# Graph layers on one core: the expansion's f32 products become three bf16 products each

## The reference

```python
def _spmm(row, col, vals, x):
    msg = vals[:, None] * x[col]
    return jax.ops.segment_sum(msg, row, num_segments=N)

def _layer(x_prev, row, col, vals, W_a, b_a, W_b, b_b):
    h = _spmm(row, col, vals, x_prev)
    z = (h + x_prev) @ W_a.T + b_a + h * x_prev @ W_b.T + b_b
    return jnp.where(z >= 0, z, NEG_SLOPE * z)
x = emb[x_ids]
x1 = _layer(x, ...)
x2 = _layer(x1, ...)
x3 = _layer(x2, ...)
return jnp.concatenate((x, x1, x2, x3), axis=1)
```

## Time and profile before

| | |
|---|---|
| median of 3 runs | 9204.5 us (9197.29 to 9209.96) |
| the profiled execution, its own time | 9172.53 us |
| its span, first to last instruction | 9170.8 us |
| mean granted clock of PE | 0.967 of 2.4 GHz |
| PE busy, share of the span | 8540.0 us, 93% |
| PE's weight loads (PEld) | 7869.9 us, 86% |
| DVE busy | 7440.7 us, 81% |
| POOL busy | 5280.1 us, 58% |
| ACT busy | 4551.0 us, 50% |
| DMA | 1718.93 MB, mean 187 GB/s |

### The profile page before, as it was taken

The page is one execution under the profiler, slowest core; times in us unless marked ns, Lnnn a source line. Parts: engine busy times, 40 slices in busy tenths (PEclk is TensorE's granted clock), DMA queues, the critical chain, the costliest instruction groups (busy, mean ns, idle before and its releaser), DMA issues.

```text
span 9170.8 us, 229058 instructions
## 1 busy us (share of the span) xinstructions
PE 8540.0 (93%) x69832; PEld 7869.9 (86%) x69833; DVE 7440.7 (81%) x11531; ACT 4551.0 (50%) x14200; POOL 5280.1 (58%) x3637
## 2 busy tenths in 40 slices
PE   7799997899995899999999999999999999999999
PEld 4577775677773799999999999999999999999999
DVE  7799996999996888877777788777777888777777
ACT  0799991699993466611112566511112566511112
POOL 8688781488783122278886122288885222388884
PEclk8899998899996899999999999999999999999999
DMA  2211110111119877788886677788887677788886
GB/s 84 38 7 7 7 7 16 11 7 7 7 7 28 189 281 280 279 283 283 285 285 241 233 279 280 276 285 285 285 285 220 252 280 281 277 283 283 285 285 202
DMA packets 1005650, 1718.93 MB, mean 187 GB/s; under 512 B 378356, under 2 KB 429624, under 8 KB 1004920
## 3 DMA queue, kind: packets, MB, share of 16 engines
q0 software_dynamic: 378656, 958.17, 34.9%
q1 hardware_dynamic: 499680, 751.43, 22.6%
q10 hardware_dynamic: 127224, 8.24, 3.2%
HBM read 961.68 MB, written 755.66 MB: 187 GB/s over the span
## 4 chain that ended last, share of the span: by engine, by line
PE 63%; DVE 2%; ACT 2%; issue 1%; DMA 1%; DVEq 0%; ACTq 0%; SPq 0%; POOL 0%; POOLq 0%
PE ps L955 35%; PE ps L946 25%; ACT work L717 2%; DVE hT L1272 1%; PE ps L963 1%; PE ps L983 1%; PE ps L984 1%; DVE work L1325 0%; PE ps L973 0%; ACTq L722 0%; DVEq L1329 0%; DVE work L1210 0%; DMA work<-messages,work 0%; DMA tile_base<-start_base 0%; DMA work<-tile_base 0%
## 5 line engine op out<-in xcount | busy, mean ns | idle before, releaser
L955 PE MATMUL ps<-work 128*128 128x125 f32 x28416 | 3294.0, 278 | 44.3 <-DVE work L1325 40.8
L955 PEld LDWEIGHTS ps<-work 128*128 128x128 f32 x28416 | 3240.0, 192 | 98.3 <-DVE work L1325 65.9
L551 POOL DMA_INDIRECT work<-messages,work x1776 | 2712.7, 1527 | 636.4 <-issue 631.7
L946 PE MATMUL ps<-xb,work 125*128 x21504 | 2450.5, 276 | 96.3 <-ACT work L717 75.9
L946 PEld LDWEIGHTS ps<-xb,work 125*128 125x128 f32 x21504 | 2419.3, 192 | 127.4 <-issue 127.4
L1325 DVE TENSOR_TENSOR work<-work,iota_p 128x1000 f32<-128x1000 f32 x1776 | 2119.5, 1193 | 35.3 <-ACT work L735 35.3
L717 ACT ACTIVATE work<-ps,work 128x128 f32<-128x128 f32 x5376 | 1532.8, 368 | 1113.5 <-PE ps L946 1113.5
L536 POOL PARTITION_BROADCAST work<-work x672 | 556.1, 829 | 2324.9 <-DMA work<-slot_cols 1260.7
L735 ACT ACTIVATE work<-work 128x8 f32<-128x8 f32 x1776 | 534.4, 301 | 2687.2 <-DMA work<-messages,work 2685.5
L843 PEld LDWEIGHTS ps<-hT 128*128 128x128 f32 x12768 | 1485.0, 196 | 302.2 <-ACT stage L648 182.7
L843 PE MATMUL ps<-hT 128*128 128x96 f32 x12768 | 1521.3, 280 | 191.2 <-ACT stage L648 188.0
(11 more groups left out here) (206 smaller groups left out, 4054.5 us busy)
## 6 DMA issues: line engine op xcount, KB each, us to landing
messages<-work SPq DMA_DIRECT2D x2688, 256.0 KB, 2.4
work<-messages,work POOLq DMA_INDIRECT x1776
out_x<-xb SPq DMA_DIRECT2D x150, 125.0 KB
sorted_edges<-stage,run_idx POOLq DMA_INDIRECT x798
work<-slot_cols SPq DMA_DIRECT2D x672, 2.0 KB
work<-lane_places SPq DMA_DIRECT2D x532, 5.2 KB
out_x<-xb ACTq DMA_DIRECT2D x4, 1562.5 KB
sorted_edges<-hT SPq DMA_DIRECT2D x4, 908.0 KB
```

The costliest lines, as they stand in the source:

```text
L551: pool.indirect_dma_start(out=ck[:, n, :, :].rearrange("p h x -> p (h x)"), out_offset=None, in_=flat, in_offset=bass.IndirectOffsetOnAxis ...
L946: last = t.matmul(ps[:, n % PR, j * D:(j + 1) * D], col_hot[:, n % OHR, j * P:(j + 1) * P], x_flat[:, bass.ds(offs[n], D)], start=True, st ...
L955: last = t.matmul(part[n], ck[:, n, j // CH, j % CH * D:(j % CH + 1) * D], sel[:, n % SELB, j, :], start=j == 0, stop=j == CHB - 1)
```

## The change

The f32 product of a 0/1 matrix with rows of x becomes three bf16 products that add up in PSUM. An f32 value is split into three bf16 pieces whose sum is exactly the value: `x_high` is the upper half of each f32 of `xb`, read where it lies (a bf16 view at a step of two); `rest` = x - x_high is written in f32 into `hT`, and its upper half `x_mid` is read in place in the same way; `x_low` = rest - x_mid is written packed, in bf16, into `work`. DVE makes `rest` and `x_low` at the start of each layer in four parts each (SPLITS), and PE waits for all of them (`pieces_ready`).

The 0/1 matrices and the column numbers (in DRAM, in `col_src` and in `col_row`) are bf16. DVE makes the matrices of two groups in one instruction, the ring holds eight groups (three pairs ahead of PE), and `col_row` is a ring of two rows (CR2) instead of four, so that POOL waits for the matrices of the row before the last. Since `hT` holds `rest` during the expansion, it isn't zeroed piece by piece: one memset of 12500 columns follows the last group of a layer, and the block sums wait for it. Some sizes of the work buffer follow from this.

```diff
...
-LEAD = 3
...
+CR2 = 2
...
-ZC = 224
+HSORT = 12544
+HTW = NB * D
+SPLITS = 4
...
-        slot_cols = dram("slot_cols", [SLOTS2], U8)
+        slot_cols = dram("slot_cols", [SLOTS2], BF16)
...
-        hT = sb("hT", [P, ABODIES * ZC])
+        hT = sb("hT", [P, HTW])
...
-        OHR = 4
+        OHR = 8
...
-        col_hot = work[0:BLK, AOH0:AOH0 + OHR * GE].rearrange("c (n s) -> c n s", n=OHR)
-        MSG0 = AOH0 + OHR * GE
...
+        x_flat = xb[:, :, :].rearrange("r n d -> r (n d)")
+        rest = hT[0:BLK, 0:HTW]
+        x_high = x_flat.bitcast(BF16).rearrange("r (e t) -> r e t", t=2)[:, :, 1]
+        x_mid = rest.bitcast(BF16).rearrange("r (e t) -> r e t", t=2)[:, :, 1]
+        x_low = wb[0:BLK, 2 * LO0:2 * LO0 + HTW]
...
-        col_row = wu[:, 4 * CV0:4 * CV0 + CB * BATCH * GE].rearrange("c (h x) -> c h x", h=CB)
+        col_row = wb[:, 2 * CV0:2 * CV0 + CR2 * BATCH * GE].rearrange("c (h x) -> c h x", h=CR2)
...
-        slot_col = wu[0:DP, 0:SPP]
+        slot_col = wb[0:DP, 0:SPP]
...
                 def spread_cols(i, first):
                     for h in range(CB):
                         pool.wait_ge(col_src_in[h], la * (ABODIES * DMA) + i * DMA + DMA)
-                        if not first:
-                            pool.wait_ge(col_hot_ready, la * GROUPS + i * AU + ((h + 1) * BATCH - AU))
+                        if not first or h >= CR2:
+                            pool.wait_ge(col_hot_ready, la * (GROUPS // 2) + i * (AU // 2) + (h + 1 - CR2) * BATCH // 2)
                         taken_up()
-                        g.partition_broadcast(col_row[:, h, :], col_src[h * 32:h * 32 + 1, :], channels=P).then_inc(col_spread[h], 1)
+                        g.partition_broadcast(col_row[:, h % CR2, :], col_src[h * 32:h * 32 + 1, :], channels=P).then_inc(col_spread[h], 1)
 
...
             with pe.Fori(0, LAYERS) as la:
                 pe.wait_ge(xb_ready, la * DSTEPS + 1)
+                pe.wait_ge(pieces_ready, la * SPLITS + SPLITS)
                 pe.sem_inc(pe_layers, 1)
                 with pe.Fori(0, ABODIES) as i:
                     _, offs = nc.values_load_multi_w_load_instructions(
                         group_at[0:1, bass.ds(i * AU, AU)], engines=[mybir.EngineType.PE],
                         min_val=0, max_val=(NB - 1) * D, skip_runtime_bounds_check_because="the table holds offsets of blocks")
                     for n in range(AU):
-                        pe.wait_ge(col_hot_ready, la * GROUPS + i * AU + (n + 1))
+                        if n % 2 == 0:
+                            pe.wait_ge(col_hot_ready, la * (GROUPS // 2) + i * (AU // 2) + (n // 2 + 1))
                         pe.wait_ge(msg_ready[n % 2], la * (GROUPS // 2) + i * (AU // 2) + (n // 2 + 1))
                         for j in range(CH):
-                            last = t.matmul(ps[:, n % PR, j * D:(j + 1) * D], col_hot[:, n % OHR, j * P:(j + 1) * P],
-                                            x_flat[:, bass.ds(offs[n], D)], start=True, stop=True)
+                            at = n % OHR * GE + j * P
+                            for k, piece in enumerate((x_high, x_mid, x_low)):
+                                last = t.matmul(ps[:, n % PR, j * D:(j + 1) * D], col_hot[:, at:at + P],
+                                                piece[:, bass.ds(offs[n], D)], start=k == 0, stop=k == 2)
                         last.then_inc(expanded, 1)
 
                 with pe.Fori(0, BBODIES) as i:
...
             with dve.Fori(0, LAYERS) as la:
                 v.tensor_copy(b_now[:, :], bias[:, 0, bass.ds(la, 1)])
                 v.tensor_copy(w_now[:, :, :], w_sb[:, bass.ds(la, 1), :, :].rearrange("p a k d -> p (a k) d")).then_inc(w_now_ready, 1)
+                dve.wait_ge(x0_got, NB * DMA)
+                dve.wait_ge(xb_ready, la * DSTEPS + 1)
+                W = HTW // SPLITS
+                for c in range(SPLITS):
+                    at = slice(c * W, (c + 1) * W)
+                    v.tensor_tensor(rest[:, at], x_flat[:, at], x_high[:, at], ALU.subtract).then_inc(rest_ready, 1)
+                dve.wait_ge(slots_stored, DMA)
+                for c in range(SPLITS):
+                    at = slice(c * W, (c + 1) * W)
+                    dve.wait_ge(rest_ready, la * SPLITS + (c + 1))
+                    v.tensor_tensor(x_low[:, at], rest[:, at], x_mid[:, at], ALU.subtract).then_inc(pieces_ready, 1)
+
                 def free_message(i, n, first):
 
                     if n >= MR:
                 def make_hot(i, n):
                     if n % BATCH == 0:
                         dve.wait_ge(col_spread[n // BATCH], la * ABODIES + i + 1)
-                    dve.wait_ge(expanded, la * GROUPS + i * AU + (n + 1))
-                    v.tensor_scalar(col_hot[:, n % OHR, :], col_row[0:BLK, n // BATCH, n % BATCH * GE:(n % BATCH + 1) * GE],
+                    dve.wait_ge(expanded, la * GROUPS + i * AU + (n + 2))
+                    v.tensor_scalar(col_hot[:, n % OHR * GE:(n % OHR + 2) * GE],
+                                    col_row[0:BLK, n // BATCH % CR2, n % BATCH * GE:(n % BATCH + 2) * GE],
                                     iota_c[0:BLK, :], None, ALU.is_equal).then_inc(col_hot_ready, 1)
 
                 def expand(i, first, last_body):
-                    for n in range(AU):
-                        if n + LEAD < AU:
-                            make_hot(i, n + LEAD)
+                    for n in range(0, AU, 2):
+                        m = n + OHR - 2
+                        if m < AU:
+                            make_hot(i, m)
                         elif not last_body:
-                            make_hot(i + 1, n + LEAD - AU)
-                        if n % 2:
-                            dve.wait_ge(expanded, la * GROUPS + i * AU + (OHR + n + 1))
-                            free_message(i, n, first)
-                            v.tensor_tensor(msg[:, n % MR, :].rearrange("p (j d) -> p j d", j=CH),
-                                            ps[:, n % PR, :].rearrange("p (j d) -> p j d", j=CH),
-                                            val_of[:, bass.ds(i * (AU * CH) + n * CH, CH)][:, :, None].to_broadcast([P, CH, D]),
-                                            ALU.mult).then_inc(msg_ready[1], 1)
-                    v.tensor_scalar(hT[:, bass.ds(i * ZC, ZC)].rearrange("p (a z) -> p a z", a=2),
-                                    iota_p[:, 0:ZC // 2][:, None, :].to_broadcast([P, 2, ZC // 2]), 0.0, None, ALU.mult).then_inc(h_zeroed, 1)
-
-                for n in range(LEAD):
+                            make_hot(i + 1, m - AU)
+                        dve.wait_ge(expanded, la * GROUPS + i * AU + (OHR + n + 2))
+                        free_message(i, n + 1, first)
+                        v.tensor_tensor(msg[:, (n + 1) % MR, :].rearrange("p (j d) -> p j d", j=CH),
+                                        ps[:, (n + 1) % PR, :].rearrange("p (j d) -> p j d", j=CH),
+                                        val_of[:, bass.ds(i * (AU * CH) + (n + 1) * CH, CH)][:, :, None].to_broadcast([P, CH, D]),
+                                        ALU.mult).then_inc(msg_ready[1], 1)
+
+                for n in range(0, OHR - 2, 2):
                     make_hot(0, n)
                 expand(0, True, False)
                 with dve.Fori(1, ABODIES - 1) as i:
                     expand(i, False, False)
                 expand(ABODIES - 1, False, True)
+                dve.wait_ge(expanded, la * GROUPS + (OHR + GROUPS))
+                v.memset(hT[:, 0:N], 0.0).then_inc(h_zeroed, 1)
 
...
-                dve.wait_ge(h_zeroed, la * ABODIES + ABODIES)
+                dve.wait_ge(h_zeroed, la + 1)
```

More of the change, by code:

```diff
@@ L94 @@
 CQ = 2
-ZC = 224
-assert ABODIES * ZC >= N and ABODIES * ZC == 12544 and TB == 592 and GROUPS % AU == 0 and AU == CB * BATCH and AU % MR == 0
+HSORT = 12544
+HTW = NB * D
+SPLITS = 4
+assert HTW >= N
+assert HSORT <= HTW and TB == 592 and GROUPS % AU == 0 and AU == CB * BATCH and AU % MR == 0
 UNITS = [P, GE]
@@ L110 @@
 ROUND = 12582912.0
+WORKW = 22032
 def graph_layers(nc, ids, row, col, vals, emb, weights, biases, out):
@@ L129, in graph_layers @@
         tile_base = dram("tile_base", [P, TBW])
-        slot_cols = dram("slot_cols", [SLOTS2], U8)
+        slot_cols = dram("slot_cols", [SLOTS2], BF16)
         messages = dram("messages", [CHUNKS + CHB // CH, CH * D + CH])
-        hT = sb("hT", [P, ABODIES * ZC])
+        hT = sb("hT", [P, HTW])
         xb = sb("xb", [BLK, NB, D])
-        work = sb("work", [P, 20560])
+        work = sb("work", [P, WORKW])
         w_sb = sb("w_sb", [P, LAYERS, 2, D])
@@ L198, in graph_layers @@
         iota_bl = wb[:, 2 * IB0:2 * IB0 + OHW].rearrange("p (b l) -> p b l", l=LANES)
-        assert IB0 + OHW // 2 <= 20560
+        assert IB0 + OHW // 2 <= WORKW
         hot = [hb[:, r * LT:(r + 1) * LT] for r in range(HR)]
@@ L210, in graph_layers @@
         in_slot = hT[:, IS0:IS0 + SLOTW].rearrange("p (l c) -> p l c", c=SLOTS)
```

(28 more changed lines are left out.)

1 line of the change is left out of this document (removed).

## The result

The changed kernel takes **9031.67 us** (median of 4 runs, 9028.89 to 9040.14) beside 9202.31 us of the kernel before on the same chip: a ratio of 0.982, with a 95% interval of 0.9808 to 0.9832. It is 171 us faster, inside the range of 8670 to 9095, where a gain of 413 us was forecast.

The account below looks back on a forecast made before the run. PE was taken to bound the expansion, DVE at 85% behind it. Expansion -495, passes +76 and zeroing +6 gave -413 us: 8760 us profiled, 8792 us median; range 8670 to 9095 us.

Parts of the forecast that it names:

- PE's own share: Expansion: 12 bf16 matmuls a group replace 8 f32 records, at 56 ns each; 10.8 us a body instead of 14.6.
- Rival (b): Expansion: weight loads don't hide at 2.4 GHz, 87 ns a matmul, 17.2 us a body, 9648 us; chance 0.10.
- (c): Expansion: two pieces read at a 4-byte step run at half rate, 107 ns; 17.8 us a body, 9749 us; chance 0.05.
- The hole: PE between two bodies: about 2.5 us without issue, 1.55 us covered by queued matmuls, 0.95 us idle.
- rival (a): Expansion: PE sees the whole 2.5 us hole, or broadcasts stop DVE; 13.3 us a body or more, 8993 us; chance 0.20.
- DMA: Expansion's stores: the DMA engines' floor is 0.705 us a group, 11.3 us a body.
- the expansion's term: Three expansions: 168 bodies of 12.1 us, 2033 us, 495 us less than before.
- the column reads: Expansion's DMA: the doubled column reads, 4 KB for four groups, are nothing beside the stores' 256 KB a group.
- DVE, POOL, SP: Expansion, a body: DVE 9.8 to 12.2 us with POOL's broadcasts of 1.4 us; SP 11.3 us, at most 12.1.
- Between the stages: Before each expansion: DVE's eight passes take 27.9 us, adding 28 us in layer 1, 24 in layers 2 and 3; 76 in all.
- The zeroing: After each layer's last message: one DVE memset of 10.8 us, mostly hidden in DVE's idle time; 6 us for three layers.

Follow-up runs that it names:

- e9: The changed kernel with offsets loaded once a layer and SP storing 64 of 512 message columns in layers 2 and 3: 8704.52 us (one run).
- e2: The changed kernel with PE's loop in bodies of 32 groups, one load of 32 offsets each: 9105.36 us, ratio 0.9908.
- e3: The changed kernel with DVE writing 64 of the 1024 columns of each pair of 0/1 matrices: 9024.92 us (one run).
- e4: The changed kernel with SP storing 64 of 512 message columns in layers 2 and 3: 8865.14 us (one run).
- e5: The changed kernel with a body's 16 offsets loaded four at a time: 8872.21 us, ratio 0.9664.
- e8: The changed kernel with a body's 16 offsets loaded eight at a time: 8904.44 us, ratio 0.9701.
- e1: The changed kernel with PE's 16 offsets loaded once a layer instead of once a body: 8878.34 us, ratio 0.9658.
- e7: e1 with only the first of the three bf16 products, x_high: 8760.01 us (one run).
- e10: e5 with the four passes that write x_low made twice at each layer's start: 8919.77 us, ratio 0.9715.

## Why the prediction was right in direction and wrong in size

**PE's own share: right.** "So I take 128/2.4 = 53 ns plus 3, 56 ns". Matmuls stand 57 to 58 ns apart at 2.4 GHz, and e9 with PE full gives 630 us/10752 = 58.6 ns, gaps and all: 11.26 us a body against 10.8. Rival (b) at 87 ns and (c), half the rate for a strided piece, are out: the three groups that read `xb`, `hT` and `work` last 223, 222 and 221 ns a matmul, and the next one starts 58, 58 and 55 ns after them on the mean: reading at a step of 4 bytes costs 3 ns at most. The Trainium skill (TensorE: Matmul & The Clock Gate, Back-to-back issue gap) names about 81 ns for such a stream; the 58.6 ns of e9 disagree.

**The hole: this step failed.** The prediction said "If again some 2.3 groups are ahead, at 0.67 they cover 1.55 us, and 0.95 us stay". In the body shown above, the trace of PE's sequencer has the branch at the body's end at 3309.32, the load at 3309.72 and the next matmul at 3312.46: a hole of 3.14 us, of which PE's work covers 0.91, to 3310.23; before, 3216.82, 3217.21 and 3219.26, a hole of 2.44 us with 1.90 covered. So two things were wrong, and each costs the same: 0.64 us less cover than the 1.55 forecast, and 0.64 us more hole than 2.5. First, what waits ahead of PE is a number of instructions and not of groups: 15 records of a matmul with their weight loads when the branch begins, 17 before, though a group now has 12 and not 8. The other bodies agree: while the load runs, a median of 9 matmuls start in the changed kernel, in e2, e3 and e4 alike, and 13 in the kernel before. In groups the cover is 1.25 where it was 2.1, and in time 0.9 us, since each matmul is half as long. Second, the load grew from 1.55 to 2.3 us because faster groups bring denser stores (the DMA share while the load runs is 0.95 instead of 0.75); e4 shows the cause. PE idles 2.2 us a body instead of 0.95, which is 70 us a layer. And the longer idle brings 48 to 51 us an expansion at 1.2 GHz, in which some 460 matmuls start about 106 ns apart instead of 58; that costs some 20 us. In e4, e5 and e8, with idle stretches of about 1.05, 0.6 and 0.85 us, the window's clock is 1.00; with 2.2 it is 0.97, with e2's 4.5 it is 0.92. The prediction gave the clock no price. The three terms make up the body: 192 x 0.058 = 11.1, 2.2 idle and 0.4 for the clock are the 13.7 us measured.

This is rival (a) (13.3 us a body, 8993 us), which had 0.20: the whole hole of 2.5 us seen. It was closer than the forecast, but for half the reason: some of the hole is covered, and the hole is longer. That its 8993 us lie so near the 9031.67 is luck, since the two errors nearly cancel.

**DMA: the floor was set too low.** "0.705 us a group is their floor, 11.3 us a body". The busy time of a group holds (0.90 of 0.794 us is 0.715 in e1; 0.94 of 0.753 us is 0.71 in e7), but the share that a stage reached is 0.90 to 0.94, not 1: 12.0 us a body with PE's work cut to a third, 12.7 with all of it. So even with no hole the forecast's 12.1 was out of reach for this kernel. At 2033 us forecast and 2294 measured, the expansion's term is off by 262 us. e1 puts about 160 of it on the load and its clock (3 x 53); the rest is the stores' floor of 12.7 instead of 12.1, 3 x 34 = 102.

The trace of e1 shows more of where the missing tenth goes. Five to seven stores are under way nearly all the time, and between dips the share is 1.0 with some 380 GB/s. The dips go with the column loads: of what the share lacks in 600 us, 87% lies between 1 us before and 0.5 us after the packet of such a load, stretches that make up 46% of the time. On the mean of 182 loads that is 0.3 us each, four times a body, 1.2 of the 1.4 us between 11.3 and 12.7. A deep one, around a packet at 3402.48 us:

```profile
3401.50:3402.00 0.50, 0.50 (x12) 0.50 (x10) 0.50 (x1) 0.50 (x3) 0.50 (x1) 1.00 1.02 385
3402.00:3402.50 0.50, 0.50 (x13) 0.50 (x11) 0.50 (x2) 0.49 (x2) 0.23 (x1) 1.00 0.31 90
3402.50:3403.00 0.50, 0.50 (x12) 0.47 (x10) 0.50 (x2) 0.16 (x1) 0.00 (x0) 1.00 0.14 49
3403.00:3403.50 0.50, 0.50 (x12) 0.50 (x11) 0.49 (x2) 0.50 (x3) 0.00 (x0) 1.00 1.03 381
```

The prediction called the column reads "nothing beside that", by their bytes. That they cause the dips is not shown: no run took them away, and none changed the eight message buffers or the order in which SP issues.

**DVE, POOL, SP: right, as far as they were tested.** A broadcast takes 1.30 us (1.4 forecast), two groups' matrix 0.48 us alone and up to 1.5 beside a broadcast, 0.65 on the mean: 8 x (0.65 + 0.69) = 10.7 us, inside "9.8 to 12.2". e9 runs SP's body in 11.26 us, so the 12.1 of its upper bound is out.

**Between the stages: right, a little low.** +86.5 us for 76. The passes take 27.4 us (27.9 forecast), and e10 shows that all of a pass is paid for; in layer 1 the forecast's 28 holds (27.9), in layers 2 and 3 its 24 were 29.4 and 29.2; in layers 2 and 3 DVE starts them 2.5 us after its copy, and the first four passes take 15.62 us instead of 13.69 while POOL's broadcasts of the columns run beside them, which the prediction had left out. The zeroing costs 10.47 us (10.8 forecast) and starts 2.55 us after the last message: +7.4 for 6.

**Not foreseen:** the block sums are 5 to 6 us a layer shorter in the changed kernel (1094 to 1096 us) than in the two built on the old one (1099 to 1101); the other changed kernels agree (1094 to 1097) but for the first layer of e1, with 1100. The distances of over 0.15 us between two of PE's matmuls there take 36 us a layer beyond the usual 0.112, where they took 42. No run here took that apart, and its cause stays open. So do the 6 us by which the medians of e10 and e5, taken on two chips, lie further apart than the passes make.

## What to carry to other kernels

Count the cover of a stall on a sequencer in queued instructions times their new length, not in groups of work: making PE twice as fast halves what hides its own register loads. Split such a load so that each piece fits under that cover (4 x 0.58 us instead of 2.3 took the ratio from 0.982 to 0.966 here, some 144 us, and the old kernel from 1 to 0.987, 120 us). Merging two of them into one took it from 0.982 to 0.991. When a stage speeds up, ask what its denser DMA traffic will stretch, and don't take 1 as the share that DMA can reach: 256 KB stores with small loads among them reached 0.90 to 0.94 here.

## What the runs showed of the hardware that was not expected

- PE's load of registers from SBUF costs 0.07 us a register with DMA at 0.20 (1.106 us for 16, e4), 0.097 us with a share of 0.75 while it runs (1.55 us for 16, the kernel before), and 0.145 us with one of 0.88 to 1.02 (0.58, 1.17, 2.3 and 4.5 us for 4, 8, 16 and 32).
- A bf16 matmul of 128 columns with its weight load goes every 58.6 ns for a whole expansion (e9). With the moving operand packed the next start follows after 55 ns, with one read at a step of 4 bytes after 58.
- Stores of 256 KB with a column load of 4 KB after every fourth reach a DMA share of 0.90 and 331 GB/s (landing after 4.9 us, e1), and 0.94 and 346 GB/s when PE has a third of the work (e7); the share is 1.0 between dips that come with the column loads.
- The waits view put 91 us on DVE's matrices where PE's sequencer was busy loading; the row "weight load <- issue" had it right.
